# Pair sums of a recommendation tower: one matmul of 128 rows per sum, or two of 64 rows

## The reference

```python
e = stack([tbl_f[ids[:, f]] for f in range(32)], axis=1)       # 2048 x 32 x 64
z = sum(e, axis=-1)                                            # 2048 x 32
outer = einsum('bpd,pde,bpe->bp', e[:, II], kernels, e[:, JJ]) # 2048 x 496
h = concatenate([z, outer, dense_ctx], axis=1)                 # 2048 x 544
h = maximum(h @ W_top1 + b_top1, 0)                            # 512
h = maximum(h @ W_top2 + b_top2, 0)                            # 256
y = h @ W_top3                                                 # 2048 x 1
```

## Time and profile before

| what | value |
|---|---|
| median of 3 runs | 874.92 us (874.81 to 875.81) |
| the profiled execution | 875.68 us, span 873.9 us |
| granted TensorE clock | 1.000 |
| PE busy | 840.1 us, 96% |
| VectorE busy | 623.2 us, 71% |
| ScalarE busy | 151.9 us, 17% |
| GpSimd busy | 494.5 us, 57% |
| DMA | 28.32 MB, mean 32 GB/s |

### The profile page before, as it was taken

How to read it: one execution, slowest core, us unless ns; L and a number is a source line. 1 busy time by engine, 2 the same in 40 slices (tenths; PEclk the granted TensorE clock), 3 DMA queues, 4 the chain that set the end, 5 groups by cost and what they waited for, 6 DMA issues and landing times.

```text
span 873.9 us, 15786 instructions
## 1 busy us (share of the span) xinstructions
PE 840.1 (96%) x6584; PEld 404.9 (46%) x6584; DVE 623.2 (71%) x706; ACT 151.9 (17%) x273; POOL 494.5 (57%) x550
## 2 busy tenths in 40 slices
PE   1899999999999999999999999999999999999997
PEld 1788888766655333333333333333333333333332
DVE  0677577688866788888855488888845588888840
ACT  1212312212210220020210320020211312020001
POOL 7875777777777777777776477667723430000000
DMA  9511111111111111111111011111100000000000
GB/s 325 187 28 23 28 31 29 28 28 31 28 28 27 28 27 27 30 28 27 28 26 25 17 25 26 23 27 27 26 12 13 16 14 1 1 1 1 1 1 1
DMA packets 24209, 28.32 MB, mean 32 GB/s; under 512 B 13254, under 2 KB 13385, under 8 KB 24012
## 3 DMA queue, kind: packets, MB, share of 16 engines
q0 software_dynamic: 16384, 16.81, 10.7%
q1 hardware_dynamic: 7744, 10.49, 3.6%
q10 hardware_dynamic: 12, 0.01, 0.0%
HBM read 27.27 MB, written 0.01 MB: 31 GB/s over the span
## 4 chain that ended last, share of the span: by engine, by line
PE 92%; DVE 3%; POOL 2%; DMA 1%; issue 1%; ACT 1%; DVEq 0%; ACTq 0%
PE y L615 50%; PE acc L632 26%; PE y L662 7%; PE y L598 4%; PE y L678 3%; DVE prod L563 3%; POOL rows L369 2%; PE y L667 1%; DMA rows<-tbl,ids_sb 1%; PE y L688 1%; POOL spare L368 1%; DMA ids_sb<-ids 0%; ACT h_in L445 0%; PE y L644 0%; ACT h L482 0%
## 5 line engine op out<-in xcount | busy, mean ns | idle before, releaser
L563 DVE TENSOR_TENSOR prod<-y,xt 128x1024 f32<-128x1024 f32 (+2 forms) x600 | 582.4, 1033 | 199.4 <-PE y L615 198.3
L369 POOL DMA_INDIRECT rows<-tbl,ids_sb x512 | 483.4, 944 | 214.0 <-issue 111.2
L615 PE MATMUL y<-xt,kw 64*128 64x512 f32 (+2 forms) x2976 | 476.9, 463 | 4.3 <-DVE prod L563 3.2
L615 PEld LDWEIGHTS y<-xt,kw 64*128 64x128 f32 x2976 | 244.0, 190 | 217.0 <-issue 199.4
L632 PE MATMUL acc<-prod,ones_strip 128*32 128x512 f32 (+2 forms) x2976 | 239.4, 454 | 0.3 <-DVE prod L563 0.3
L632 PEld LDWEIGHTS acc<-prod,ones_strip 128*32 128x32 f32 x2976 | 79.4, 109 | 142.4 <-issue 68.1
L414 ACT COPY xt<-y 128x1024 f32<-128x1024 f32 (+3 forms) x56 | 36.2, 646 | 300.8 <-PE y L598 300.7
L662 PE MATMUL y<-h_in,w_sb 128*128 128x512 f32 (+2 forms) x192 | 58.4, 457 | 3.1 <-ACT h_in L445 2.6
L598 PE MATMUL y<-ident,rows 128*128 128x128 f32 x256 | 41.4, 289 | 20.5 <-DMA rows<-tbl,ids_sb 20.4
L535 DVE TENSOR_REDUCE z_rows<-rows 128x8 f32<-128x512 f32 (+2 forms) x96 | 44.6, 500 | 17.2 <-DMA rows<-tbl,ids_sb 17.2
L445 ACT COPY h_in<-acc 128x512 f32<-128x512 f32 (+2 forms) x24 | 10.6, 443 | 240.4 <-PE acc L632 240.4
(11 more groups left out here) (22 smaller groups left out, 55.1 us busy)
## 6 DMA issues: line engine op xcount, KB each, us to landing
rows<-tbl,ids_sb POOLq DMA_INDIRECT x512
kw<-pair_k SPq DMA_DIRECT2D x14, 512.0 KB, 11.9
w_sb<-w SPq DMA_DIRECT2D x1, 1024.0 KB, 12.2
w_sb<-w SPq DMA_DIRECT2D x1, 512.0 KB, 13.6
kw<-pair_k SPq DMA_DIRECT2D x1, 384.0 KB, 18.3
ids_sb<-ids SPq DMA_DIRECT2D x1, 256.0 KB, 2.7
kw<-pair_k SPq DMA_DIRECT2D x1, 256.0 KB, 4.2
w1z_sb<-w1z SPq DMA_DIRECT2D x1, 256.0 KB, 12.3
```

Source lines behind the costliest of these rows:

```text
L369: pool.indirect_dma_start(out=rows[:, s, c, h, :], out_offset=None, in_=tables[f], in_offset=bass.IndirectOffsetOnAxis(ap=ids_sb[:, b, f:f ...
L563: nc.vector.tensor_tensor(prod_part(t, d, n), y_part(t, d, n), x, ALU.mult).then_inc(y_read, n)
L615: last = nc.tensor.matmul(y[:, h, :], kw[part, d, :], xt[part, slot_of(t, units[h][0] // 2), 0:w], start=True, stop=True)
```

## The change

Each unit's sum is made by two matmuls, one for each target: 64 rows by 32 columns, on the upper and on the lower half of the array's rows. They write into different banks: the accumulator is now one tensor of two banks, bank n for target n. `ones_strip` has one column of ones over all 128 rows. A chunk holds 128 units, that is 64 steps, and a tile has two chunks; both banks are in use in every chunk, so the first sum of a chunk waits until the chunk just before it is copied (`acc_read`, c instead of c - 1). ScalarE copies both banks with one instruction of 128x1024. The first layer reads the same number of 128-row pieces as before (two chunks of two banks instead of four of one), with its weights laid out to match.

```diff
-STRIPS = 16
+STRIPS = 32
...
-        h_in = sb("h_in", [P, CHUNKS, TILE])
+        h_in = sb("h_in", [P, CHUNKS, 2, TILE])
...
-        w1_sb = sb("w1_sb", [P, CHUNKS, N1])
+        w1_sb = sb("w1_sb", [P, CHUNKS, 2, N1])
...
-        ones_strip = sb("ones_strip", [P, 62])
+        ones_strip = sb("ones_strip", [P, 63])
...
-        accs = [bank(f"acc{i}", [P, TILE]) for i in range(2)]
+        accs = bank("accs", [P, 2, TILE])
...
-                nc.scalar.copy(h_in[:, c, 0:w], accs[(CHUNKS * t + c) % 2][:, 0:w]).then_inc(acc_read, 1)
+                nc.scalar.copy(h_in[:, c, :, 0:w], accs[:, :, 0:w]).then_inc(acc_read, 1)
...
-            dve.memset(ones_strip[0:DIM, 30:31], 1.0).then_inc(consts_made, 1)
-            dve.memset(ones_strip[DIM:P, 31:32], 1.0).then_inc(consts_made, 1)
+            dve.memset(ones_strip[:, STRIPS - 1:STRIPS], 1.0).then_inc(consts_made, 1)
...
-                if first % CHUNK_STEPS == 0 and c >= 2:
+                if first % CHUNK_STEPS == 0 and c >= 1:
 
-                    pe.wait_ge(acc_read, c - 1)
+                    pe.wait_ge(acc_read, c)
 
                 pe.wait_ge(y_read, N_STEPS * t + end)
                 for u in range(2 * first, 2 * end):
                     q, s = unit_place(u)
-                    last = nc.tensor.matmul(acc[32 * q:32 * q + 32, 0:w], ones_strip[:, 30 - 2 * s:62 - 2 * s],
-                                            prod_part(t, u // 2)[:, u % 2, :],
-                                            start=s == 0, stop=ends_chunk(t, g) and u >= 2 * end - QUADRANTS)
+                    for n in range(2):
+                        part = slice(DIM * n, DIM * n + DIM)
+                        last = nc.tensor.matmul(accs[32 * q:32 * q + 32, n, 0:w],
+                                                ones_strip[part, STRIPS - 1 - s:2 * STRIPS - 1 - s],
+                                                prod_part(t, u // 2)[part, u % 2, :], start=s == 0,
+                                                stop=ends_chunk(t, g) and u >= 2 * end - QUADRANTS)
...
-                        nc.tensor.matmul(y[:, h, 0:w], w1_sb[:, c, j * P:(j + 1) * P], h_in[:, c, 0:w],
-                                         start=c == 0, stop=False)
+                        for n in range(2):
+                            nc.tensor.matmul(y[:, h, 0:w], w1_sb[:, c, n, j * P:(j + 1) * P], h_in[:, c, n, 0:w],
+                                             start=c == 0 and n == 0, stop=False)
```

More of the change, by code:

```diff
@@ L57 @@
 UNITS = 2 * N_STEPS
-CHUNKS = -(-N_STEPS // (2 * STRIPS))
 CHUNK_STEPS = 2 * STRIPS
+CHUNKS = -(-N_STEPS // CHUNK_STEPS)
 PAIRS = FIELDS * (FIELDS - 1) // 2
@@ L622, in sum_group @@
                 c = CHUNKS * t + first // CHUNK_STEPS
-                acc = accs[c % 2]
                 w = WIDTHS[t]
-                if first % CHUNK_STEPS == 0 and c >= 2:
-                    pe.wait_ge(acc_read, c - 1)
+                if first % CHUNK_STEPS == 0 and c >= 1:
+                    pe.wait_ge(acc_read, c)
                 pe.wait_ge(y_read, N_STEPS * t + end)
@@ L690, in mlp3 @@
                 last.then_inc(y_full, 1)
-            pe.wait_ge(consts_made, 3)
+            pe.wait_ge(consts_made, 2)
             for what, t, n in PLAN:
@@ L735 @@
     k = np.zeros((P, N_STEPS, P), pair_k.dtype)
-    w1 = np.zeros((CHUNKS, P, N1), w_top1.dtype)
+    w1 = np.zeros((CHUNKS, 2, P, N1), w_top1.dtype)
     for d, step in enumerate(STEPS):
@@ L743 @@
                 k[DIM * h:DIM * h + DIM, d, DIM * n:DIM * n + DIM] = pair_k[pair] if i < f else pair_k[pair].T
-                w1[u // (QUADRANTS * STRIPS), 32 * q + 2 * s + n] = w_top1[FIELDS + pair]
+                w1[u // (QUADRANTS * STRIPS), n, 32 * q + s] = w_top1[FIELDS + pair]
     w1z = np.zeros((P, N1), w_top1.dtype)
@@ L754 @@
         dram_in("pair_k", k.reshape(P, N_STEPS * P)),
-        dram_in("w1", w1.transpose(1, 0, 2)),
+        dram_in("w1", w1.transpose(2, 0, 1, 3)),
         dram_in("w1z", w1z),
```

## The result

The changed kernel takes 892.91 us (891.02 to 893.64, 4 runs), the kernel before beside it 875.37 us: a ratio of 1.0197, 95% interval 1.0179 to 1.0215. The direction was forecast, the size was not: +17.5 us instead of +5.6, a hair over the upper end of the range.

What follows compares the result with a forecast made beforehand. TensorE's own stream was taken as the bound, its array work unchanged. Later starts 3.3 + 0.2, tiling changes 0.4 and the wider copy 1.7 gave +5.6 us on 874.92, so 880.5 us; range 866 to 892.

Steps and rivals of the forecast that it cites:

- The array work: Sum blocks on TensorE: twice the instructions, eight places side by side, still four waves of 0.43 us; no change.
- Edge 1 at 256 and 512 samples: Start of wide sum blocks: the last of eight places starts 28 ns later; 3.3 us over 117 groups, some narrow.
- Edge 1 at 128 samples: Narrow sum blocks: 28 ns each, plus 0.2 us for the second tile's second waves; first tile hidden beside gathers.
- Rival B: Starts at 128 samples can't go faster than 29 ns: 1.88 us more a group, 895 to 910 us; chance 0.05.
- Edge 2, the change between blocks: Borders between steps and sums still cost 0.11 us, no gain; sums before the last layer at four places lose 0.4 us.
- Rival A: Change between step and sum blocks gets cheap when rows stay at 64: 854.8 us, or 867.7 for one border; chance 0.15.
- Edge 3, the copy: At each tile's end the first layer waits for ScalarE's copy, now twice as wide: 1.7 us in all.
- The new wait: Mid-tile, the second chunk's first sum waits for ScalarE's copy: hidden under a step block with 2.5 us to spare.
- The sum: All terms over the whole kernel: +5.6 us, giving 880.5 us, bounds 877 to 885.

Runs made afterwards that it cites:

- Experiment 5: Kernel before and changed kernel, each with the first layer working off copied chunks before waiting for the last chunk's copy: 872.91 and 887.01 us.
- local: Changed kernel with each unit's sum in the two 128-sample tiles again one matmul of 128 rows by 32 columns: 879.24 us, ratio 1.0045.
- (1): Changed kernel with only the narrow (128-sample) tiles' sums put back to 64 instructions a block: 879.24 us.
- (2): Changed kernel and kernel before, each with groups of 8 steps (two buffers instead of four) in the 128-sample tiles: 880.0 and 877.37 us.
- (4): Kernel before and changed kernel, each with every sum of the two 128-sample tiles issued twice: 902.3 and 942.0 us.
- (3, 4): 3: changed kernel with 128 waits, met at once, ahead of TensorE's first instruction to move later code, 891.52 us; 4: see (4).
- double_after: Changed kernel with every sum of the two 128-sample tiles issued twice, in blocks of 256 instructions: 942.0 us, ratio 1.0761.
- half_before: Kernel before with groups of 8 steps in the 128-sample tiles: 877.37 us, ratio 1.0021.
- half_late_2: Kernel before with groups of 8 steps in the 128-sample tiles and the first layer's later wait for the last chunk's copy, run again: 874.48 us.
- half_late_lead_2: Kernel of half_late_2 with gathers of later tiles released 72 instead of 56 full-width steps ahead, run again: 874.68 us, ratio 0.9992.
- late_before: Kernel before with the first layer working off copied chunks before waiting for the last chunk's copy: 872.91 us, ratio 0.9967.
- half_after: Changed kernel with groups of 8 steps (two buffers instead of four) in the 128-sample tiles: 880.0 us, ratio 1.0056.

## Why the prediction was right and wrong

**The array work** (right). Four waves of eight, 0.43 us each, at 512 and 256 samples.

**Edge 1 at 256 and 512 samples** (right). Forecast 28 ns a block, measured 1.878 - 1.854 = 24 ns as the mean of the 59 mid-tile blocks at 512 samples, which agree to 3 ns, and 23 ns at 256.

**Edge 1 at 128 samples** (the step that failed). I priced these blocks like the wide ones, 28 ns and 28 ns more for the second wave, 0.05 us, and only the eight of the second tile; the sixteen lost 0.76 us each on average, 12.1 us. The gathers of the first tile hid nothing: its eight blocks lost 5.4 us, and the second tile's first sums came 5.9 us later. It is Rival B, with chance 0.05 and a price of 20 to 35 us, that came true at about 12. My argument against it was that 16 loads and matmuls in 56 ns fit a wave of 107. But 7 ns is the distance of starts within a wave, at the head of a block, and I used it as if it were the rate at which instructions reach TensorE. The rows had only an upper bound for a matmul's share of that, 29 ns, and the change asked for half of it, 13.7. Between these nothing was known. In place of one rate the runs show the first 50 to 100 matmuls of a block at the full pace, and a stop where a border of 256 instructions comes up too soon after a transfer. The six gaps at such borders are 5.7 of the 12.1 us. Hops and slower waves make up the rest. Over longer stretches of dense sums Rival B's figure was about right: 27 to 31 ns a matmul between two waited-for borders. The cost stayed below its price since a narrow block has only 128 of them and the steps behind it are slower work, under which code can arrive. The page of before showed the instruction queue, and I hadn't read it.

**Edge 2, the change between blocks** (right, Rival A is wrong). The border between 64x128 and 64x32 costs what the others cost: the last start of a sum block to the next block is as before, and the sums before the last layer now pay for it, 1.88 instead of 1.74 us. The Trainium skill ("TensorEngine Tiling (Array Packing)", Key Properties) has a drain for every change of mode; the trace agrees, with 0.11 us at this new border too (0.14 less the 0.024 of Edge 1).

**Edge 3, the copy** (right). Forecast 0.43 us at each 512-sample tile, measured 0.65, 0.47 and 0.44 beyond the spread of starts; 0.25 at 256 (forecast 0.21). Experiment 5 confirms it in the wide tiles from the other side.

**The new wait** (right). No wait on the accumulator shows in the middle of a tile: all mid-tile sum blocks at 512 samples take 1.88 us.

**The sum.** With the narrow tiles put back, +3.4 to +3.9 us was measured where my terms without the 0.4 us for narrow blocks give +5.2. The trace of local has 4.7 us more in its wide sums, as forecast; 0.6 us of it are taken back by a shorter wait for gathers near 235, and another 0.7 at the start of the first tile, which I had at nothing. So the miss is the narrow blocks, and the other terms were right or slightly too high in their effect.

What is shown: the loss is in the narrow blocks (1), depends on their length (2) and not on the array's pace (4), and its long gaps, 5.7 of 12.1 us, stand at borders of 256 instructions, 1.22 to 1.55 us behind the end of a transfer of code (3, 4). What is argued: that the hops of 0.09 to 0.18 us are supply as well; the blocks of half the length have fewer of them, but they stand at no fixed place of the code. What stays open: what makes these hops, and why 127 waits more are only 63 instructions more in the trace.

## What to carry to other kernels

A split into smaller matmuls can leave the array's time alone, as here, and doubles the instructions of that part. Before doing it, divide the shortest block's time by its instructions, not the average over the kernel, and compare that with the densest stretch that the trace has shown without a break; the distance of starts within a wave is no evidence for it. If the stretch is longer than 256 instructions, look also at how long each 256 of them last beside the transfers of code. And where an engine waits for a copy of the last of several pieces, begin with the pieces that are there.

## What the runs showed of the hardware that I had not expected

TensorE ran 128 loads and matmuls at 13.8 ns a pair behind a gap (double_after). Its code comes in transfers of 16 KB, 256 instructions each, that take 0.9 to 1.6 us, and where one was waited for, work went on 1.22 to 1.55 us after its end (38 gaps). With two such waits in one block the 128 pairs between them took 3.5 to 4.0 us. The Trainium skill ("Runtime: NRT & Kernel Launch", Instruction fetch mechanics) has the blocks of 16 KiB and 256 instructions, as the trace does, and says that crossing a border is mostly hidden; here it was in the kernel before, and in the changed one six of the 25 borders in the narrow tiles cost a gap of 0.5 to 1.5 us.

In a wait of 4.2 to 4.5 us for gathers the granted clock fell from 1.0 to 0.5 (1.2 GHz) and stayed there for 6.8 us (half_before, half_late_2, half_late_lead_2); waits of 0.7 to 1.4 us at the same place left it at 1.0 (before, late_before, half_after).

Eight places of 64x32, in two banks of the same partitions and accumulating, run side by side at 512 samples as four of 128x32 do: 1.88 against 1.85 us a block, about what the later start of the last of eight explains (24 ns, 28 forecast).
